# Combination of the experts and projections of layer 1: gathers counted by chunk, remainders on GpSimd, two store slots, rows written into X

## The reference, cut to what matters

```
x = layernorm(x + prob0 * expert_row0 + prob1 * expert_row1)     # combination, each token's two experts
q = rope(x @ wq);  lat = x @ w_down
k = rope(lat @ wk_up);  v = lat @ wv_up                          # 16 heads of 16
```

## Time and profile before

| | |
|---|---|
| time before, median of 3 runs | 4770.78 us (4746.70 to 4777.87) |
| the profiled execution | 4747.15 us, span 4745.4 us |
| stage F, from POOL's first memset to the first instruction of attention G | 1944.05 to 2207.22 us |
| of it, DVE waiting for the first combination | until 1989.72 us |
| of it, chunks | 1989.72 to 2192.72 us |
| busy in the chunks (203.3 us) | PE 140.4, DVE 145.1, ACT 53.5, POOL 33.0 us |

### The profile page before, as it was taken

The page is one execution under the profiler, slowest core; times in us unless marked ns, Lnnn a source line. Parts: engine busy times, 40 slices in busy tenths (PEclk is TensorE's granted clock), DMA queues, the critical chain, the costliest instruction groups (busy, mean ns, idle before and its releaser), DMA issues. The chain is left out here.

```text
span 4745.4 us, 81148 instructions
## 1 busy us (share of the span) xinstructions
PE 3974.7 (84%) x24868; PEld 2674.6 (56%) x24868; DVE 3008.8 (63%) x6137; ACT 2507.5 (53%) x4350; POOL 1541.1 (32%) x2118
## 2 busy tenths in 40 slices
PE   5999999962699999473999999966979798979798
PEld 2544444432699999331544444435767676757676
DVE  1888778822354454273887778826967554967656
ACT  1477677740354454121577677743556554546554
POOL 2232223214200000411111112115979502979700
PEclk8799889986899999786799999988989899989999
DMA  7322223132212111246132223223456311456511
GB/s 174 93 58 34 33 36 48 22 110 82 81 54 91 53 58 49 92 146 129 31 46 46 47 49 59 38 88 132 154 169 181 112 40 68 153 158 184 159 54 45
DMA packets 333300, 410.24 MB, mean 86 GB/s; under 512 B 41308, under 2 KB 242478, under 8 KB 330125
## 3 DMA queue, kind: packets, MB, share of 16 engines
q1 hardware_dynamic: 289868, 270.15, 17.9%
q0 software_dynamic: 38464, 131.41, 13.7%
q10 hardware_dynamic: 4608, 4.20, 0.3%
HBM read 248.58 MB, written 156.19 MB: 85 GB/s over the span
## 5 line engine op out<-in xcount | busy, mean ns | idle before, releaser
L606 DVE TENSOR_REDUCE G_mpart<-G_pm 128x1 f32<-128x512 f32 (+3 forms) x1024 | 618.1, 651 | 193.3 <-PE G_pm L495 185.6
L606 DVE TENSOR_REDUCE B_mpart<-B_pm 128x1 f32<-128x512 f32 (+3 forms) x1024 | 618.0, 651 | 167.1 <-PE B_pm L495 159.3
L585 ACT ACTIVATE G_p<-G_psc 128x1024 f32<-128x1024 f32 (+1 forms) x576 | 532.5, 976 | 145.8 <-PE G_psc L532 143.6
L585 ACT ACTIVATE B_p<-B_psc 128x1024 f32<-128x1024 f32 (+1 forms) x576 | 532.4, 977 | 137.1 <-PE B_psc L532 134.9
L495 PE MATMUL G_pm<-G_ks,G_qs 48*128 48x512 f32 (+3 forms) x1664 | 459.7, 417 | 105.0 <-DMA G_ks<-G_one 58.7
L495 PE MATMUL B_pm<-B_ks,B_qs 48*128 48x512 f32 (+3 forms) x1664 | 457.4, 414 | 73.8 <-DMA B_ks<-B_one 42.2
L495 PEld LDWEIGHTS G_pm<-G_ks,G_qs 48*128 48x128 f32 x1664 | 247.8, 208 | 419.6 <-DVE G_mpart L606 216.6
L1868 POOL TENSOR_SCALAR J_pr<-J_pr,J_rc 128x256 f32<-128x256 f32 x512 | 462.4, 926 | 66.0 <-DVE J_rc L2013 65.9
L495 PEld LDWEIGHTS B_pm<-B_ks,B_qs 48*128 48x128 f32 x1664 | 245.1, 203 | 389.0 <-DVE B_mpart L606 217.3
L510 PE MATMUL G_po<-G_p,G_v 128*32 128x512 f32 (+3 forms) x2560 | 314.7, 576 | 0.1
L510 PE MATMUL B_po<-B_p,B_v 128*32 128x512 f32 (+3 forms) x2560 | 312.3, 572 | 1.3 <-POOL B_p L357 1.2
(11 more groups left out here) (301 smaller groups left out, 7855.4 us busy)
## 6 DMA issues: line engine op xcount, KB each, us to landing
J_v<-lve SPq DMA_DIRECT2D x64, 520.0 KB, 4.0
J_k<-lkT SPq DMA_DIRECT2D x64, 512.0 KB, 5.3
lve<-I_v SPq DMA_DIRECT2D x64, 260.0 KB, 2.1
lqT<-I_tT SPq DMA_DIRECT2D x64, 256.0 KB, 2.4
lkT<-I_tT SPq DMA_DIRECT2D x64, 256.0 KB, 2.8
J_q<-lqT SPq DMA_DIRECT2D x64, 256.0 KB, 4.3
ein<-B_z SPq DMA_DIRECT2D x32, 307.0 KB
E_xin<-ein POOLq DMA_DIRECT2D x8, 1152.0 KB, 6.2
```

What stands on the lines that cost most here:

```text
L585: act.activation(p[:, t % PSLOTS, 2 * pr:2 * pr + 2, span(t)], psc[:, 2 * pr:2 * pr + 2, span(t)], ACT.Exp, scale=SC).then_inc(e_done[pr], 1)
L606: dve.tensor_reduce(mpart[:, heads[0] % 2, a:z, qb, kc], pm[slots[e]][:, 0:len(heads) * w].rearrange("p (h k) -> p h k", k=w), AX, ALU.max ...
```

## The change

- POOL (L1274 to L1299 of the changed kernel): gathers are counted by chunk (`got[n]`, 8 for each). The 16 of chunks 0 and 1 go first. Those of chunk n+2 are issued two by two, each pair ahead of one remainder of chunk n.
- The remainders move from DVE to POOL (`low`). DVE keeps the products and the sum; products run one round ahead of the sum, with two slots each for `F_t1`, `F_t2`, and four for `F_r`.
- `F_hi` and `F_lo` have two slots of four rounds, counted by `stored[n % 2]`; v has its own count (`v_stored`). SP stores v first and then each round as its remainder is done.
- DVE writes the normalized rows into X, and PE transposes from X. ACT's copy and `F_xn` are gone.
- PE does the values between round 0 and round 1, and the transposes of the next chunk between rounds 1 and 2. ACT evicts the values ahead of the square root of the next chunk, and evicts the transposes between roundings 1 and 2.
- All loops over the chunks are written out. In the combination the 4 + 4 multiply-adds are followed by one wait for each four; in most chunks of before, each was.

```diff
+    NCK, PER = TOK // CH, SUB * TOPK
...
-        t1 = sb("t1", [P, CH], F32)
-        t2 = sb("t2", [P, CH], F32)
-        r = sb("r", [P, 2, CH], F32)
-        hi = sb("hi", [P, RJ, CH], F32R)
-        lo = sb("lo", [P, RJ, CH], F32R)
+        t1 = sb("t1", [P, 2, CH], F32)
+        t2 = sb("t2", [P, 2, CH], F32)
+        r = sb("r", [P, RJ, CH], F32)
+        hi = sb("hi", [P, 2, RJ, CH], F32R)
+        lo = sb("lo", [P, 2, RJ, CH], F32R)
...
-            for b in range(B):
-                with eng.Fori(0, CPB - 1) as c:
-                    body(b * CPB + c, b, c, b * CPB + c + 1)
-                n = b * CPB + CPB - 1
-                body(n, b, CPB - 1, n + 1 if b < B - 1 else None)
-
-        def chunks(eng, body):
-            with eng.Fori(0, B) as b:
-                with eng.Fori(0, CPB) as c:
-                    body(b * CPB + c, b, c)
 
         @block.gpsimd
         def _(pool):
             pool.memset(eps[:], EPS).then_inc(eps_set, 1)
             pool.memset(v[:], 1.0).then_inc(eps_set, 1)
-            for b in range(B):
-                for q in range(QT):
-                    for k in range(TOPK):
-                        pool.indirect_dma_start(Y[:, b * QT + q, k], None, eout,
-                                                bass.IndirectOffsetOnAxis(slot_g[:, b, k, q:q + 1], 0),
-                                                bounds_check=E_ * ROWS - 1, oob_is_err=False).then_inc(got[b], 16)
+
+            def gather(n, at, end):
+                for x in range(at, end):
+                    tile, k = n * SUB + x // TOPK, x % TOPK
+                    pool.indirect_dma_start(Y[:, tile, k], None, eout,
+                                            bass.IndirectOffsetOnAxis(slot_g[:, tile // QT, k, tile % QT:tile % QT + 1], 0),
+                                            bounds_check=E_ * ROWS - 1, oob_is_err=False).then_inc(got[n], 16)
+
+            def low(n, j):
+                wait_apart(pool, hi_done, n * RJ + j + 1, fence)
+                if n >= 2:
+                    wait_apart(pool, stored[n % 2], n // 2 * (2 * RJ * 16), fence)
+                pool.tensor_tensor(lo[:, n % 2, j], r[:, j], hi[:, n % 2, j].bitcast(F32), ALU.subtract).then_inc(lo_done, 1)
+
+            gather(0, 0, PER)
+            gather(1, 0, PER)
+            for n in range(NCK):
+                for j in range(RJ):
+                    if n + 2 < NCK:
+                        gather(n + 2, j * PER // RJ, (j + 1) * PER // RJ)
+                    low(n, j)
...
+            turn(0)
+            for n in range(NCK):
+                latent(n)
+                rotated(n, 0)
+                values(n)
+                rotated(n, 1)
+                if n + 1 < NCK:
+                    turn(n + 1)
+                rotated(n, 2)
+                rotated(n, 3)
...
-                act.wait_ge(n_done, n + 2)
-                act.activation(X[:, ds(n * SUB, SUB), :],
-                               xn[:], ACT.Copy).then_inc(x_copied, 1)
...
+            def high(n, j):
+                act.wait_ge(r_done, n * RJ + j + 2)
+                if n >= 2:
+                    act.wait_ge(stored[n % 2], n // 2 * (2 * RJ * 16) + 1)
+                act.activation(hi[:, n % 2, j], r[:, j], ACT.Copy).then_inc(hi_done, 1)
+
+            deviation(0)
+            turned(0)
+            for n in range(NCK):
+                latent(n)
+                values(n)
+                if n + 1 < NCK:
+                    deviation(n + 1)
+                high(n, 0)
+                high(n, 1)
+                if n + 1 < NCK:
+                    turned(n + 1)
+                high(n, 2)
+                high(n, 3)
...
+            def combine(n):
+                dve.wait_ge(got[n], 16 * PER)
+                if n >= 1:
+                    dve.wait_ge(n_done, n + 1)
...
-                dve.wait_ge(x_copied, n + 1)
-                dve.wait_ge(t_done, n + 1)
+                ch.end()
                 for s in range(SUB):
-                    last = dve.tensor_scalar(xn[:, s], y[:, s], mv[:, s, 0:1], rs[:, s:s + 1], ALU.subtract, ALU.mult)
-                    if s == SUB - 1:
-                        last.then_inc(n_done, 1)
-                    else:
-                        ch.link(last)
-                ch.end()
-
-            def body(n, b, c, nxt):
-                if nxt is not None:
-                    first(nxt)
-                cj.start(n)
+                    last = dve.tensor_scalar(X[:, n * SUB + s], y[:, s], mv[:, s, 0:1], rs[:, s:s + 1], ALU.subtract, ALU.mult)
+                last.then_inc(n_done, 1)
+
+            def products(n, j):
+                q, cols = n * RJ + j, slice(n % CPB * CH, (n % CPB + 1) * CH)
+                dve.wait_ge(r_mm, q + 2)
+                if q >= 2:
+                    dve.wait_ge(r_done, q)
+                dve.tensor_tensor(t1[:, j % 2], pb[3 + 2 * (j % 2)][:], co[:, cols], ALU.mult)
+                dve.tensor_tensor(t2[:, j % 2], pb[4 + 2 * (j % 2)][:], si[:, cols], ALU.mult).then_inc(r_read, 1)
+
+            def rotated(n, j):
+                q = n * RJ + j
+                dve.wait_ge(r_read, q + 4)
+                if n >= 1:
+                    dve.wait_ge(lo_done, q - RJ + 2)
+                dve.tensor_tensor(r[:, j], t1[:, j % 2], t2[:, j % 2], ALU.add).then_inc(r_done, 1)
+
+            combine(0)
+            for n in range(NCK):
+                if n + 1 < NCK:
+                    combine(n + 1)
+                products(n, 0)
                 for j in range(RJ):
-                    dve.wait_ge(r_mm, n * RJ + j + 2)
-                    main, swap = pb[3 + 2 * (j % 2)], pb[4 + 2 * (j % 2)]
-                    dve.tensor_tensor(t1[:], main[:], co[:, ds(c * CH, CH)], ALU.mult)
-                    last = dve.tensor_tensor(t2[:], swap[:], si[:, ds(c * CH, CH)], ALU.mult)
-                    last.then_inc(r_read, 1)
-                    dve.wait_ge(r_read, n * RJ + j + 4)
-                    dve.tensor_tensor(r[:, j % 2], t1[:], t2[:], ALU.add).then_inc(r_done, 1)
-                    dve.wait_ge(hi_done, n * RJ + j + 2)
-                    last = dve.tensor_tensor(lo[:, j], r[:, j % 2], hi[:, j].bitcast(F32), ALU.subtract)
-                    cj.link(last)
-                dve.sem_inc(lo_done, 1)
-                cj.end()
-            skewed(dve, first, body)
-            dve.wait_ge(x_copied, TOK // CH + 1)
+                    if j + 1 < RJ:
+                        products(n, j + 1)
+                    rotated(n, j)
+            dve.wait_ge(n_done, NCK + 1)
...
+            for n in range(NCK):
+                b, c = n // CPB, n % CPB
                 sp.wait_ge(v_done, n + 2)
                 for s in range(SUB):
-                    sp.dma_start(vs_v[ds(b, 1), ds(c * CH + s * P, P)].rearrange("o t g e -> (o t) g e"),
-                                 v[:, s]).then_inc(stored, 16)
-            chunks(sp, body)
-            sp.wait_ge(stored, 16 * STORES * (TOK // CH) + 1)
+                    sp.dma_start(vs_v[b, c * CH + s * P:c * CH + (s + 1) * P], v[:, s]).then_inc(v_stored, 16)
+                for j in range(RJ):
+                    sp.wait_ge(lo_done, n * RJ + j + 2)
+                    for dst, src in (((qh, hi), (ql, lo)) if j < KC else ((kh, hi), (kl, lo))):
+                        row = b * D + j % KC * P
+                        sp.dma_start(dst[row:row + P, c * CH:(c + 1) * CH], src[:, n % 2, j].bitcast(F32)
+                                     ).then_inc(stored[n % 2], 16)
```

96 lines of the change are left out of this document (36 added, 60 removed).

## The result

| | before | after |
|---|---|---|
| median of 20 runs | 4762.15 us (4736.94 to 4785.46) | 4731.71 us (4696.62 to 4782.98) |
| profiled execution, span | 4745.4 us | 4729.8 us |
| stage F, POOL's first memset to attention G's first | 263.2 us | 232.3 us |

The ratio is 0.9926, 95% interval 0.9909 to 0.9943: 0.74% faster. The ratio leaves out two slower executions of the changed kernel, over 1.5% above its fastest, which the medians include. The medians lie 30.4 us apart and stage F is 30.9 us shorter. The spans of the profiled executions differ by 15.6 only, because the other stages, whose code is the same, vary. Over the fourteen kernels profiled for this study stage F begins between 1926.1 and 1960.8, and from its end to the end of the span it takes 2538 to 2577 us, in no relation to the edits.

The account below looks back on a forecast made before the run. Stage F was taken as a chain through several engines, none full, with DVE pacing the chunks. 25.5 - 11.8 + 8.4 - 2.1 + 6.4 = 26.4 us gained; 4770.8 - 26 = 4745 us, range 4699 to 4775.

Parts of the forecast that it names:

- the ring: Bursts 0 to 6: DVE's burst, POOL's remainders and gather pairs, then combination make periods of 26.2 us; 11.8 us lost over six.
- the lock: DVE's sums, with two SBUF inputs, wait for POOL's remainders to end: about 4 us in all in bursts 6 and 7.
- the early start: Ahead of chunk 0, which now needs 8 gathers: burst 0 starts at 1985.5, not 2010.98, 25.5 us gained.

## What to carry to other kernels

When work is moved to another engine's queue, follow the ring through that queue: here a gather that DVE wants one period later stood behind work which DVE's next burst releases, and issuing it one chunk earlier was worth 38 us while the move itself was worth nothing. Before moving a two-input subtraction from VectorE to GpSimd beside other two-input VectorE work, count the lock as part of the price. Test the cheapest part of a change alone: the early start, without the rest and with the gathers held back, gave all that the whole change gave.
